# Routed experts in 24 steps of four experts with 32 rows each, one expert's weights read in place, expert numbers read ahead of the loop

## What is computed

```python
def _grouped_mm(a, w, group_sizes):
    return jax.lax.ragged_dot(a, w, group_sizes)

def _swiglu(x, gw, uw, dw):
    return jax.nn.silu(x @ gw) * (x @ uw) @ dw
```

## Time and profile before

| | us |
|---|---|
| median of 3 runs | 726.79 |
| the three runs | 723.13, 726.79, 728.34 |
| the profiled execution | 722.07 |
| its span (first to last instruction) | 720.2 |
| mean granted PE clock over the span | 0.946 of full speed |

### The profile page before, as it was taken

How to read it: one execution, slowest core, us unless ns; L and a number is a source line. 1 busy time by engine, 2 the same in 40 slices (tenths; PEclk the granted TensorE clock), 3 DMA queues, 4 the chain that set the end, 5 groups by cost and what they waited for, 6 DMA issues and landing times. The chain is left out here.

```text
span 720.2 us, 14244 instructions
## 1 busy us (share of the span) xinstructions
PE 608.4 (84%) x5188; PEld 354.6 (49%) x5189; DVE 527.7 (73%) x979; ACT 367.1 (51%) x598; POOL 313.7 (44%) x286
## 2 busy tenths in 40 slices
PE   3767787999999999999997878789998895779991
PEld 3244555667667666675675645222322243524440
DVE  5768888898887988888986556977776366447762
ACT  0323342675665666756656434048566773037660
POOL 2774546545464455647564144132000100727762
PEclk9779999999999999999999999789999999789996
DMA  8322010101010110101100715155933500112224
GB/s 258 75 65 85 16 31 9 30 17 23 17 23 20 28 23 18 23 17 31 25 16 16 141 51 112 26 124 178 250 126 117 206 3 0 41 45 65 71 61 135
DMA packets 31872, 47.15 MB, mean 65 GB/s; under 512 B 5520, under 2 KB 21948, under 8 KB 30524
## 3 DMA queue, kind: packets, MB, share of 16 engines
q1 hardware_dynamic: 30268, 43.09, 22.5%
q0 software_dynamic: 1536, 3.16, 1.3%
HBM read 29.12 MB, written 9.46 MB: 54 GB/s over the span
## 5 line engine op out<-in xcount | busy, mean ns | idle before, releaser
L618 POOL TENSOR_TENSOR rnorm<-ssum_c,neg_half 128x16 f32<-128x16 f32 x32 | 94.3, 2946 | 108.4 <-DVE ssum_c L1021 106.8
L630 POOL TENSOR_TENSOR region_r<-region_b,region_d 128x512 f32<-128x512 f32 x64 | 82.7, 1314 | 38.7 <-DVE region_b L1026 38.1
L1181 DVE TENSOR_REDUCE mneg<-ps 128x2 f32<-128x1024 f32 x64 | 77.2, 1220 | 22.3 <-PE ps L1626 21.2
L848 ACT ACTIVATE region_r<-ps 128x1024 f32<-128x1024 f32 x64 | 63.0, 1023 | 34.2 <-PE ps L1642 34.1
L750 ACT ACTIVATE region_a<-ps 128x1024 f32<-128x1024 f32 x32 | 32.8, 1025 | 64.2 <-PE ps L1411 64.2
L596 POOL TENSOR_TENSOR var_eps<-mv,eps 128x4 f32<-128x4 f32 x20 | 8.0, 401 | 125.9 <-DVE mv L963 125.9
L1410 PE MATMUL ps<-region_d,hT 128*128 128x512 f32 x64 | 37.6, 672 | 20.5 <-DVE region_b L1026 19.7
L735 ACT ACT_TABLE_LOAD x39 | 50.0, 1283 | 1.4 <-PEq L1878 0.7
L1026 DVE TENSOR_TENSOR region_b<-ps,rnorm 128x1024 f32<-128x1024 f32 x32 | 39.1, 1222 | 11.8 <-POOL rnorm L618 10.9
L1524 PE MATMUL ps<-region_a,region_d 128*114 128x512 f32 x96 | 46.6, 609 | 0.6 <-ACT region_a L767 0.6
L1477 PEld LDWEIGHTS ps<-region_b,pts 128*64 128x64 f32 x512 | 32.2, 137 | 24.8 <-issue 24.8
(11 more groups left out here) (236 smaller groups left out, 1413.8 us busy)
## 6 DMA issues: line engine op xcount, KB each, us to landing
region_a<-in_wgu SPq DMA_DIRECT2D x16, 512.0 KB, 5.9
region_b<-region_a SPq DMA_DIRECT2D x56, 130.0 KB, 2.3
region_d<-in_wd SPq DMA_DIRECT2D x4, 1024.0 KB, 5.2
parts_dram<-region_b SPq DMA_DIRECT2D x6, 384.0 KB, 2.6
xs_dram<-region_a SPq DMA_DIRECT2D x1, 2064.0 KB, 8.0
pts<-xs_dram SPq DMA_DIRECT2D x32, 64.5 KB, 1.8
region_d<-in_wqkv SPq DMA_DIRECT2D x2, 768.0 KB, 8.9
region_a<-parts_dram SPq DMA_DIRECT2D x3, 384.0 KB, 6.8
```

What stands on the lines that cost most here:

```text
L618: g.tensor_tensor(rnorm[:, :], ssum_c[n % 2][:, :], neg_half[:, :], ALU.pow).then_inc(S["rnormed"], 1)
L630: g.tensor_tensor(dst, src, tab, ALU.mult).then_inc(S["rot_bb"], 1)
L848: act_(dst, bank(l1_bank[what, b, i], of=2), ACT.Exp).then_inc(T["ex"], 1)
L1181: d.tensor_reduce(mneg[b % 2][:, 2 * i:2 * i + 2], bank(l1_bank[what, b, i], of=2) .rearrange("p (q t) -> p q t", q=2), AX.X, ALU.max, neg ...
```

## The change

Groups become 32 rows (`HALF` = 32), so there are at most 2048/32 + 31 = 95 groups, and a step takes four of them (`PER` = 4): `PAIRS` = 24 steps of 128 rows. A step's `gate_up` is four matmuls of 32 stationary columns, one for each quarter of the PSUM partitions, and `down` is eight. An expert's gate, up and down weights now lie side by side, 768 wide (`wx`), and come in 16 DMAs of 768 KB. The first of a step's four experts isn't copied: PE addresses its weights by a register. DVE copies the second and third (768 wide each), ACT the fourth, into buffers four deep, freed by `down`.

All expert numbers are read before the loop: 24 on PE (`first`), 24 on ACT (`two`), and 48 on DVE (`ones`), of which 24 stand between `gate_s` and `add_s` of each of the last two sequences of the shared expert.

The number of groups is now found by three small instructions (rounding), where before a comparison and a reduction over 1024 elements stood. The expert of each group is found over 3072 elements of one partition, before over 2048. The row numbers come in one DMA of 4-byte elements (`row_ids`), so `number` goes; filler rows carry a number out of bounds and the scatter skips them.

```diff
+PER = 4
+HALF = P // PER
+SLOTS = TOK // HALF + EXP - 1
+PAIRS = -(-SLOTS // PER)
+EW = 2 * INTER + IC * P
+AHEAD, WBUF = 4, 4
...
@@ SP
-            order = (7, 8, 9, 10, 11, 12, 13, 0, 1, 5, 6, None, 2, 3, 4, None, None, None, 14, 15)
+            chunks = [2 * c for c in (5, 6, 7, 8, 11, 12, 13, 14, 15, 0, 3, 4, 1, 2, 10, 9)]
...
+                if what == "probs" and i in (0, 3, 6, 13):
...
+                    sp.dma_start(wx[:, e0:e0 + 2, :], A["wx"][:, e0:e0 + 2, :]).then_inc(M["w_x"], 16)
...
+            sp.dma_start(row_ids, xs_dram[:, P:ROW].bitcast(U32).rearrange("(j p) c -> p (j c)", p=P),
+                         allow_slow_non_contiguous=True).then_inc(M["ids_in"], 16)
             for j in range(PAIRS - AHEAD):
                 sp.wait_ge(M["xT_mm"], j + 1)
-                sp.wait_ge(M["ids"], j + 1)
...
@@ POOL
-            for j in range(NUM):
-                number(j)
+            pool.wait_ge(M["ids_in"], 16)
             for j in range(PAIRS):
-                if j + NUM < PAIRS:
-                    number(j + NUM)
-                pool.wait_ge(M["ids"], j + 1)
                 pool.wait_ge(M["y_sb"], j + 1)
...
+                                     in_=ys[j % AHEAD], in_offset=None, bounds_check=TOK - 1, oob_is_err=False)\
+                 .then_inc(ys_out[j % AHEAD], 16)
@@ ACT
             def weights_two(j, e):
 
-                need(a, M["gu_mm"], j - GBUF + 1)
-                act_(gu_pair[j % GBUF][1], wgu[:, bass.ds(e, 1), :].rearrange("p a n -> p (a n)"), ACT.Copy)\
+                need(a, M["y_mm"], j - WBUF + 1)
+                act_(w_copy[j % WBUF][2], wx[:, bass.ds(e, 1), :].rearrange("p a n -> p (a n)"), ACT.Copy)\
...
             a.wait_ge(M["x4s"], BATCH)
-            a.wait_ge(M["w_gu"], 16 * 16)
-            weights_two(0, expert_two(0))
+            a.wait_ge(M["w_x"], 16 * 16)
+            two = [expert_two(j) for j in range(PAIRS)]
+            weights_two(0, two[0])
...
@@ DVE
-            link(d.tensor_tensor(over, cnt.unsqueeze(2).to_broadcast([P, EXP, HALVES]),
-                                 consts[:, EXP:EXP + HALVES].unsqueeze(1).to_broadcast([P, EXP, HALVES]), ALU.is_gt))
-            link(d.tensor_reduce(ntile, over, AX.X, ALU.add))
+            link(d.tensor_scalar(ntile, cnt, (HALF - 1) / 2, 1.0 / HALF, ALU.add, ALU.mult))
+            link(d.tensor_scalar(ntile, ntile, ROUNDER, None, ALU.add))
+            link(d.tensor_scalar(ntile, ntile, -ROUNDER, None, ALU.add))
...
+            def experts_of(j):
+                return [v.value_load(exp_of[0:1, PER * j + w:PER * j + w + 1], min_val=0, max_val=EXP - 1) for w in range(1, 3)]
+
+            v.wait_ge(M["slots"], 2)
+            ones = []
             for b in range(SHARED_EARLY // IC + 1, BATCH):
                 for c in range(IC):
                     gate_s(IC * b + c)
+                ones += [experts_of(len(ones) + j) for j in range(PAIRS // 2)]
                 add_s(b)
...
+            def weights_one(j, experts):
+
+                need(v, M["y_mm"], j - WBUF + 1)
                 for w in range(2):
-                    last = d.tensor_copy(d_pair[j % DBUF][w], wd[:, bass.ds(pair[w], 1), :, :].rearrange("p a c n -> p (a c n)"))
+                    last = d.tensor_copy(w_copy[j % WBUF][w], wx[:, bass.ds(experts[w], 1), :].rearrange("p a n -> p (a n)"))
...
@@ PE
-                for w in range(2):
+                for w in range(PER):
                     rows = slice(w * HALF, (w + 1) * HALF)
-                    last = mm(bank(2 + j % 2)[rows, :], xsT[j % 2][:, rows], gu_pair[j % GBUF][w], start=True, stop=True,
+                    weights = wx[:, bass.ds(first[j], 1), 0:2 * INTER].rearrange("p a n -> p (a n)") if w == 0 else \
+                        w_copy[j % WBUF][w - 1][:, 0:2 * INTER]
+                    last = mm(bank(2 + j % 2)[rows, :], xsT[j % 2][:, rows], weights, start=True, stop=True,
...
             pe.wait_ge(M["x4s"], BATCH)
+            pe.wait_ge(M["slots"], 2)
+            pe.wait_ge(M["w_x"], 16 * 16)
+            first = [pe.value_load(exp_of[0:1, PER * j:PER * j + 1], min_val=0, max_val=EXP - 1) for j in range(PAIRS)]
             tokens_T(0)
```

More of the change, by code:

```diff
@@ L209, in build @@
         m1, m2 = region_r[:, 2048:2560], region_r[:, 2560:3072]
[L210 to L213, removed]
+        m3 = region_r[0:1, 3072:3072 + PER * PAIRS * EXP]
+        rows_in = [pts[1][:, i, :] for i in range(AHEAD)]
         xsT = [region_r[:, 5632 + i * P:5632 + (i + 1) * P] for i in range(2)]
@@ L219, in build, with copies @@
         warm2 = hT[1][:, 448:449]
[L220 to L226, removed]
+        row_ids = region_r[:, 1536:1536 + PAIRS].bitcast(U32)
+        rmax, rev2, esc, score, slot_f = (region_r[:, 1568 + i * TILES:1568 + (i + 1) * TILES] for i in range(5))
+        slot_i = region_r[:, 1648:1664].bitcast(U32)
+        ntile, incl, base_e = (region_r[:, 1664 + i * EXP:1664 + (i + 1) * EXP] for i in range(3))
+        exp_of_f = region_r[0:1, 1760:1760 + PER * PAIRS]
+        exp_of = region_r[0:1, 1856:1856 + PER * PAIRS].bitcast(I32)
+        def copies(*places):
+            return [region[:, at:at + EW] for region, at in places]
+        w_copy = [copies(*((region_b, 4112 + w * EW) for w in range(PER))),
+                  copies(*((region_b, 4112 + (PER + w) * EW) for w in range(PER))),
+                  copies(*((region_r, 2048 + w * EW) for w in range(PER))),
+                  copies((region_b, 0), (region_b, EW), (region_r, 0), (region_r, EW))]
         xs_dram = nc.dram_tensor("xs_dram", (SLOT_ROWS, ROW), FP).ap()
-        y_dram = nc.dram_tensor("y_dram", (AHEAD + TOK, P), FP).ap()
+        y_dram = nc.dram_tensor("y_dram", (TOK, P), FP).ap()
         base_c = region_r[:, 0:NT * 2 * DH].rearrange("p (t z d) -> p t z d", t=NT, z=2)
@@ L572, in _ @@
             for b in range(BATCH):
[L573 removed]
+                rows = y_dram[b * SEQ:(b + 1) * SEQ, :].rearrange("(t p) c -> p t c", p=P)
                 sp.dma_start(y_g[:, b * NT:(b + 1) * NT, :], rows).then_inc(gathered[b], 16)
@@ L939, in _ @@
                 if j + 3 < PAIRS:
-                    weights_two(j + 3, e)
-                if j + 4 < PAIRS:
-                    e = expert_two(j + 4)
+                    weights_two(j + 3, two[j + 3])
                 if j + 2 < PAIRS:
@@ L1755, in down @@
                 for c in range(IC):
-                    for w in range(2):
-                        at = c * P + w * HALF
-                        last = mm(bank(6 + j % 2)[w * HALF:(w + 1) * HALF, 0:P], actT[j % 2][:, at:at + HALF],
-                                  d_pair[j % DBUF][w][:, c * P:(c + 1) * P], start=(c == 0), stop=(c == IC - 1),
-                                  skip_group_check=True)
+                    for w in range(PER):
+                        rows, at = slice(w * HALF, (w + 1) * HALF), 2 * INTER + c * P
+                        weights = wx[:, bass.ds(first[j], 1), at:at + P].rearrange("p a n -> p (a n)") if w == 0 else \
+                            w_copy[j % WBUF][w - 1][:, at:at + P]
+                        last = mm(bank(6 + j % 2)[rows, 0:P], actT[j % 2][:, c * P + w * HALF:c * P + (w + 1) * HALF],
+                                  weights, start=(c == 0), stop=(c == IC - 1), skip_group_check=True)
                 last.then_inc(M["y_mm"], 1)
             pe.wait_ge(M["x4s"], BATCH)
+            pe.wait_ge(M["slots"], 2)
+            pe.wait_ge(M["w_x"], 16 * 16)
+            first = [pe.value_load(exp_of[0:1, PER * j:PER * j + 1], min_val=0, max_val=EXP - 1) for j in range(PAIRS)]
             tokens_T(0)
```

112 lines of the change are left out of this document (44 added, 68 removed).

## The result

| | before | changed |
|---|---|---|
| median, us | 725.01 (723.13 to 728.34, 4 runs) | 745.09 (742.27 to 746.44, 4 runs) |
| profiled execution, us | 722.07 | 742.27 |
| its span, us | 720.2 | 740.5 |
| mean granted PE clock | 0.946 | 0.928 |

The ratio is 1.0253 with a 95% interval of [1.0206, 1.0300]: slower, by 20.1 us between the medians. I forecast +14.3 us (+8 to +20), a median of 741.1 within 733 to 756. The same kernel was timed twice more beside the experiments: 742.32 (e5) and 737.02 (e9), which are 15.2 and 10.6 us above the medians of the kernel before in their groups. The three differences lie on both sides of the forecast.

What follows compares the result with a forecast made beforehand. PE was taken to bound the loop, with its first tile's start also counting. First tile +31.7, eight fewer steps -15.4 and tail -2.0 gave +14.3 us: median 741.1, range 733 to 756 (+8 to +20, chance 0.65).

Steps and rivals of the forecast that it cites:

- DVE's reads: Ahead of the last `add_s`: two stretches of 24 reads at 0.62 us each, ending `add_s` 18.9 us later.
- start of the first tile: Entry of the loop: reads ahead of it move PE's first token tile from 638.1 to 669.8, 31.7 us later.
- loop, first tile to last result copy: Eight steps fewer at 1.93 us each make the loop 15.4 us shorter, its entry unchanged.
- tail: After the loop: without row numbers on POOL, the last scatter comes 1.7 us behind the last but one copy, 2.0 less.
- PE's reads: Between last `add_s` and first tile: 24 reads at 0.65 us, 15.9 us with 0.25 for the first.
- the rival of dear reads on PE: A read on PE ahead of the loop costs 1.0 us (749.5 us in all) or 1.5 (761); chance 0.13.
- equal clocks of the sequencers: Alternative for reads ahead of the loop: PE's cost what ACT's do, some 0.53 us, sum 2.9 us lower.
- ACT's reads hide beside PE's: Ahead of the loop: ACT's 24 reads, at least 10.7 us, run during PE's and add nothing.
- Reads overlap: Rival: reads standing together ahead of the loop are pipelined; at 0.3 us each, -9 us, 718; chance 0.07.
- The step: In the loop: a step of four experts takes 1.93 to 1.95 us; rival of a longer step has 0.09.
- the cover of 0.4 us: In the loop: DVE's copies finish 1.5 us into a 1.93 us step; if the slack goes, steps grow by what is missing.

Runs made afterwards that it cites:

- e5: The changed kernel timed again, unchanged: 742.32 us, ratio 1.0230 to the kernel before.
- e9: The changed kernel timed a third time, unchanged: 737.02 us, ratio 1.0191 to the kernel before.
- e6: The kernel before, with only a bounds limit added on its scatter of results: 726.77 us, ratio 1.0003.
- e4: The changed kernel without the bounds limit on the result scatter, filler rows going to spare rows: 739.34 us, ratio 1.0180 to the kernel before.
- e10: Repeat of e2, the changed kernel with DVE's numbers read in the loop: 721.67 us, ratio 0.9950 to the kernel before.
- e1: The changed kernel with PE's numbers read in the loop after three ahead, ACT's and DVE's unchanged: 746.51 us, ratio 1.0301 to the kernel before.
- e7: The changed kernel with PE's and ACT's numbers read in the loop, DVE's 48 still ahead: 735.04 us, ratio 1.0129 to the kernel before.
- e8: The changed kernel with DVE and ACT reading in the loop, PE partly where it waits anyway, nine in the loop: 713.92 us, ratio 0.9823.
- e2: The changed kernel with only DVE's numbers read in the loop, two a step: 719.62 us, ratio 0.9929 to the kernel before.
- e11: Repeat of e4, the changed kernel without the bounds limit on the result scatter: 741.51 us, ratio 1.0230 to the kernel before.
- e12: e8 without the bounds limit on the result scatter: 711.70 us, ratio 0.9828 to the kernel before.
- e3: The changed kernel with all numbers, on PE, ACT and DVE, read in the loop: 715.84 us, ratio 0.9859 to the kernel before.

## Why the prediction was right

The sign and the mechanism held: DVE's reads ahead of `add_s`, then PE's in a chain ahead of its first tile, cost more than eight steps give back. The time lay within the range; the difference, +20.1 us, is at the upper edge of the +8 to +20 given and near +14.3 only when the later timings are taken in. e9 is the execution in which the forecast can be compared term by term, because its steps weren't disturbed; the first profile shows what came on top.

| term | predicted | e9 against before | changed, first profile |
|---|---|---|---|
| start of the first tile | +31.7 | +32.3 | +34.3 |
| loop, first tile to last result copy | -15.4 | -17.2 | -11.4 |
| tail | -2.0 | -1.8 | -2.6 |
| sum of the span | +14.3 | +13.3 | +20.3 |

*DVE's reads.* 0.61 us each, predicted 0.62. Two stretches of 24 reads moved the last `add_s` by 19.6 us in e9 (634.35 to 653.94), against 18.9 forecast. That these are so near is partly luck, as two things that I had left out nearly cancel. The time from the first to the second `add_s` got 3.6 us shorter, not 1.8. The work on slots gave the 1.8 that I forecast; the rest is PE's `shared_down`, for which the second `add_s` waits. Before:

```profile
613.23 3.78 PE L1587 MATMUL ps<-region_r,region_b 128*128 128x128 f32 x16 [4.30 <-DVE region_b L1144]
```

e9:

```profile
613.81 2.05 PE L1580 MATMUL ps<-region_r,region_b 128*128 128x128 f32 x16 [2.45 <-DVE region_b L1140]
```

The granted clock in it was 0.50 before, the lower of the two levels (1.2 GHz), and 1.00 in e9; PE had idled 4.30 us ahead of it before and 2.45 in e9, because DVE was done with the slots sooner. Against that, the beginning lay 2.4 us later (first `add_s` at 607.4), which has nothing to do with the reads. This point was at 606.0 to 612.0 in the twelve profiles of kernels with the change and at 605.0 and 605.3 in the two without it (e6 is the second). In e4's (611.85) PE's clock was granted at 0.84 from 590 to 612 us, in e9's at 1.00, so the clock explains some of the spread but not e9's 2.4 us. The change moves the weight DMAs about in the attention ahead of this point, for which I allowed nothing, with 2 us either way; no run puts the old ones back, so that this costs the 2 us isn't shown. That the reads are the cause of the late last `add_s` is shown by taking them away: 17.5 us in e10. In the Trainium skill, the page DMA: Bandwidth & Descriptors, section Latency and other measured facts, gives a "`tensor_load` floor" of about 600 ns. The whole read with its register instruction is near that here, 0.53 us on ACT to 0.655 on PE; the load alone is 274 to 301 ns.

*PE's reads.* 15.77 us in e9, 15.75 in the first profile, 15.9 predicted; the rival of dear reads on PE falls. The price had no row behind it: 0.65 us was a choice between 0.45 and 1.5, and that it met the measured 0.655 so closely is luck. By equal clocks of the sequencers, which the Trainium skill gives in Advanced Engine Details and Errata, section Clock Domains, I had estimated ACT's 0.53 us and 2.9 us less. The measurement decides against equal prices, not against equal clocks: the register instructions take 146 and 147 ns and the assertions 18 on both, but the load takes 301 ns on PE and 274 on ACT, and the rest lies between the instructions.

*ACT's reads hide beside PE's.* Right, and e1 measured the cover: with PE's reads gone, `gate_up` waited for ACT until 674.05.

*Reads overlap.* Falls: the chain has 0.61 us from read to read.

*Slips in the sums.* PE at 0.45 us a read gives 26.9 us for the start of the first tile and not 26.7, and 0.6 us in 24 steps are 14.4 us and not 13. Neither enters the forecast.

*The step.* `gate_up` 0.86 and `down` 0.57 us for four experts, 1.913 us in e9 for 1.93 to 1.95 predicted; PE's address instructions are covered. The loop gave 1.8 us more than forecast in e9, and 1.4 of it lie in the entry, which I had kept as it was: from the first tile to the first result copy it took 8.57 us before and 7.21 in e9, with PE's clock granted at 0.60 and 0.71 of full speed there. In the first profile the step was 2.10. The term that was mis-sized is the cover of 0.4 us: I wrote that each step grows by what is missing if that is gone, and it went, but not by slow copies or addresses. The copies took what I gave them (two on DVE 1.02 us together for 0.95, ACT's 0.85). They started up to 1 us late, because `down`'s semaphore landed late. In the kernel before, `weights_two` waited for `gu_mm`; the change made it wait for `y_mm`, and the chain's first kind of step shows ACT on the path of this semaphore. No run put the old wait back.

*The tail.* The last scatter starts 2.6 us behind the last but one result copy in e9 (721.33 and 718.72), 3.7 before and 1.7 predicted. What I missed is that a scatter now starts 1.06 us behind its copy, with 0.5 of it there only with the bounds limit (e4). The end of the span came 1.8 us sooner all the same, but not by the way that I gave: what counts is the distance from the last copy to the last scatter, 3.0 before and 2.0 now, and from that scatter's start to the end 12.9 and 12.15 us passed. So 1.0 of the 2.0 us came as forecast, and the other 0.8, behind the scatter, no experiment took apart.

**Still open** is why the semaphore lands late. In the profiles in which it does (first, e5, e7, e8), nearly all the late ones were due within 1.3 us of the start of POOL's bounds-limited scatter, and landed about 0.6 or 1.3 to 1.5 us behind that start. In e2, e9 and e10 it was due at the same phase, with the limit, and landed in time. In e6, in the group of the late ones, too. Without the limit no profile had a late `y_mm`, but e4, e11 and e12 all ran in groups in which no kernel had any. All kernels of one group with the four-expert loop agreed.

The traces show that neither the loop nor the limit is needed for such delays. In the same profiles things were late already at 631 to 638 us, when POOL issued the last of its 16 scatters of tokens, which carry no limit, and for 2 us behind them. DVE's reads in this window (duration in ns, least/median/most), in the first profile and in e9:

```profile
L1303 DVEq TENSOR_LOAD <-region_r x7: 2/302/1397, 631.8 to 637.7; - x7
```

```profile
L1303 DVEq TENSOR_LOAD <-region_r x11: 297/302/358, 631.2 to 637.6; - x11
```

And ACT's silu, which waits for a semaphore of `shared_up`, again in the first profile and in e9:

```profile
633.44 0.60 ACT L805 ACTIVATE pts<-ps 128x512 f32<-128x512 f32 x1 [1.67 <-PE ps L1556]
```

```profile
632.95 0.60 ACT L805 ACTIVATE pts<-ps 128x512 f32<-128x512 f32 x1 [1.12 <-PE ps L1556]
```

Seven reads fit in where eleven did, and the semaphore came 0.55 us later. From the second to the third `add_s` the first profile, e5 and e7 took 25.05, 24.45 and 25.86 us; e1, e4, e9 and e11, with the same 24 reads between, 22.9. In e8, whose DVE reads nothing there, the silu waited 2.24 us where e12's waited 1.12. This is also where the first profile's first tile lost the 2.0 us by which it differs from e9's. The cause is one that changes between groups and shows both ahead of the loop and in it; no run here separates it further.

## What to carry to other kernels

- A `value_load` was a serial 0.53 to 0.66 us of its engine's sequencer here. Batched ahead of the loop it stood on the path; one or two a step, placed behind instructions that the engine already holds, cost nothing on DVE (e2) and 0.45 us on PE (e3). Before moving reads, name the instruction queued behind them: here `add_s`, for which all others waited.
- When the covering work goes, the next reader comes out (ACT's in e1). Take all readers together, or count on a smaller gain.
- The four-expert form was worth its 17 us in the loop. With its reads spread out and partly under PE's waits it beats the kernel before by nearly 2%: 713.92 (e8) and 711.70 us (e12), ratios 0.982 and 0.983, both intervals below 1.

## What I had not expected of the hardware

- The same kernel on the same chip had a mean step of 2.09 us in one group and 1.91 in another (e5, e9), with one PE semaphore landing 0.73 and 0.32 us behind the matmul's start. The medians are 742.3 and 737.0. In the same profiles as this semaphore, reads on DVE's sequencer stalled too.
- A bounds limit on an indirect DMA put its start 0.5 us back on POOL (1.06 against 0.57 us behind the copy, e9 and e4), and 0.2 us in the kernel before (1.24 against 1.05, e6). Its duration stays at 1.02 us.
- A read on PE in the middle of the loop, placed behind `down`, started 0.02 us after `down`'s first matmul in every step of e3; in the step shown there the sequencer had done `down`'s address instructions 1.1 us before. PE's sequencer was therefore less far ahead of the array than my phrase "runs ahead" took for granted; it covered three address instructions (e9) but not a read. What holds it isn't shown.
